# Latent attention: the score products of an even and an odd head issued next to each other

## The reference, cut to what matters

```
q = ln @ W_q
kv = jnp.concatenate([xn @ W_kv, ln @ W_kv], axis=1)
k, v = (kv[..., :INNER], kv[..., INNER:])
...
qn = rmsnorm(q, q_gamma) * SCALE
kn = rmsnorm(k, k_gamma)
sim = jnp.einsum('bhid,bhjd->bhij', qn, kn)
sim = jnp.where(full_mask[:, None, None, :], sim, neg)
attn = jax.nn.softmax(sim.astype(jnp.float32), axis=-1).astype(sim.dtype)
out = jnp.einsum('bhij,bhjd->bhid', attn, v)
...
return out @ W_out + b_out
```

## Time and profile before

| | |
|---|---|
| profiled execution, span | 1399.5 us |
| runs | 1397.72, 1401.20, 1401.49 us |
| mean granted TensorE clock | 0.864 of full speed |
| TensorE matmuls busy | 1089.6 us (78%) |
| VectorE / ScalarE / GpSimd busy | 810.9 / 577.6 / 535.3 us |
| score products (L1332), 128 matmuls | 52.7 us busy, 514 ns each |
| latent attention, first to last score | 864.5 to 1050 us |

### The profile page before, as it was taken

One profiled execution on the slowest core, in us unless ns is written; L12 is line 12 of the kernel. 1 busy time (PEld: TensorE's weight loads), 2 busy tenths in 40 slices (PEclk: granted clock), 3 DMA queues, 4 the chain that ended last, 5 costly groups with the idle time before them and its releaser, 6 DMA issues. The chain is left out here.

```text
span 1399.5 us, 27510 instructions
## 1 busy us (share of the span) xinstructions
PE 1089.6 (78%) x8779; PEld 824.4 (59%) x8789; DVE 810.9 (58%) x1770; ACT 577.6 (41%) x1366; POOL 535.3 (38%) x654
## 2 busy tenths in 40 slices
PE   5784968966598878506999348899998689997998
PEld 3564857855366666405999224566677367776443
DVE  4556624437647787673555353445454538775876
ACT  2442325432256655342434045554541247774000
POOL 1453734447147766380000433222220247763000
PEclk9755989988699999657999758899998789997999
DMA  3453268843221111276777120000000100000000
GB/s 105 115 148 121 102 206 292 291 146 95 77 89 41 36 44 35 83 275 220 260 257 251 59 73 1 0 1 0 1 0 9 38 8 21 16 16 5 15 22 23
DMA packets 71899, 125.99 MB, mean 90 GB/s; under 512 B 15737, under 2 KB 42499, under 8 KB 71811
## 3 DMA queue, kind: packets, MB, share of 16 engines
q1 hardware_dynamic: 64131, 103.88, 22.7%
q0 software_dynamic: 7680, 20.98, 4.5%
HBM read 53.38 MB, written 25.17 MB: 56 GB/s over the span
## 5 line engine op out<-in xcount | busy, mean ns | idle before, releaser
L297 ACT ACTIVATE xnT<-bank 128x256 f32<-128x256 f32 (+1 forms) x112 | 42.0, 380 | 85.9 <-PE bank L286 85.1
L1622 DVE TENSOR_REDUCE l2x_neg_max<-bank 128x1 f32<-128x333 f32 x64 | 32.0, 503 | 74.7 <-PE bank L1334 74.5
L3064 PE MATMUL bank<-l_weights,room 128*128 x576 | 70.1, 275 | 2.3 <-DVE room L3092 2.1
L3051 PE MATMUL bank<-room,xnT 128*128 128x128 bf16 x1152 | 69.7, 221 | 0.0
L3051 PEld LDWEIGHTS bank<-room,xnT 128*128 128x128 bf16 x1152 | 67.9, 99 | 0.3
L2712 POOL DMA_DIRECT2D l_results<-keep x24 | 13.1, 546 | 139.9 <-DVE keep L2810 139.9
L2326 PE MATMUL bank<-l0f_x_high,l_weights 128*128 128x256 bf16 x256 | 44.8, 300 | 27.7 <-DVE l0f_x_low L2351 16.8
L869 PE MATMUL bank<-ident,l_weights 128*77 128x128 f32 x256 | 39.5, 296 | 32.9 <-DVE l_weights L1060 27.6
L2165 DVE SCALAR_TENSOR_TENSOR l3f_total<-bank,l3f_share,l3f_total 128x256 f32<-128x256 f32 x112 | 54.2, 484 | 15.6 <-PE bank L2083 12.0
L3064 PEld LDWEIGHTS bank<-l_weights,room 128*128 128x128 bf16 x576 | 53.9, 97 | 13.2 <-issue 3.6
L2548 PE MATMUL bank<-l0r_xT_high,l0r_placed 128*128 128x128 bf16 x640 | 61.4, 221 | 0.0
(11 more groups left out here) (435 smaller groups left out, 3409.3 us busy)
## 6 DMA issues: line engine op xcount, KB each, us to landing
xnT<-l_weights SPq DMA_DIRECT2D x24, 1024.0 KB, 5.2
l0r_placed<-l_weights SPq DMA_DIRECT2D x40, 512.0 KB, 3.3
room<-in_L_ffn_weights SPq DMA_DIRECT2D x20, 512.0 KB, 4.6
l0w_staging<-in_L_ffn_weights SPq DMA_DIRECT2D x16, 480.0 KB, 3.9
l_weights<-in_L_ffn_weights SPq DMA_DIRECT2D x16, 384.0 KB, 3.2
l0r_room<-l_rows SPq DMA_DIRECT2D x40, 128.0 KB, 2.8
l_results<-l0r_room POOLq DMA_DIRECT2D x40, 128.0 KB, 2.8
l_rows<-l_weights SPq DMA_DIRECT2D x16, 192.0 KB, 2.3
```

The lines of the kernel that those rows point to most:

```text
L297: act.activation(self.chip.xnT[:, :, span(t, P)], bank[:, 0:DIM].rearrange("p (k n) -> p k n", k=KD), ACT.Copy).then_inc(self.copied, 1)
L3051: last = pe.matmul(h_bank[u][:, m * P:(m + 1) * P], placed.parts[w][:, u, at:at + P], x[:, u, k, :], start=(s == 1), stop=(s == PARTS * KD))
L3064: last = pe.matmul(bank[:, 2 + u, 0:DIM], h[:, u, c * P:(c + 1) * P], expert_part(split[:, w, :, :], e, KD * hidden_width + c * DIM, DIM), ...
```

## The change

Instead of `scores` at every step, TensorE issues `score_pair` at the even steps: the products of head s and head s + 1 next to each other (the one on partitions 0 to 63, the other on 64 to 127), then both mask products. The wait ahead of them is for the exponents of step s - 1 instead of s - 2. At odd steps TensorE issues no score. This holds for the prologue and for the loop; VectorE, ScalarE and GpSimd keep their programs.

```
-            def scores(b, s):
-                u, h = s // L2_HEADS, s % L2_HEADS
+            def score_pair(b, s):
+                u = s // L2_HEADS
                 if s == 0:
                     pe.wait_ge(qkT_ready, 2 * TPB * b + 2 * TPB)
                     pe.wait_ge(c_kT_placed, (KD + 1) * b + KD + 1)
-                wait(pe, probs_ready, SH * b + s - 1)
-                at = slice(L2_HEAD * (h % 2), L2_HEAD * (h % 2) + L2_HEAD)
-                pe.matmul(s_bank[h % 2][:, 0:L2_KEYS], qT[at, h // 2, u * P:(u + 1) * P], kT[at, h // 2, :],
-                          start=True, stop=False)
-                pe.matmul(s_bank[h % 2][:, 0:KEYS], mask_one[at, :], mask_now[at, :],
-                          start=False, stop=True).then_inc(scores_ready, 1)
+                wait(pe, probs_ready, SH * b + s)
+                halves = [slice(L2_HEAD * n, L2_HEAD * n + L2_HEAD) for n in range(2)]
+                pair = (s % L2_HEADS) // 2
+                for n, at in enumerate(halves):
+                    pe.matmul(s_bank[n][:, 0:L2_KEYS], qT[at, pair, u * P:(u + 1) * P], kT[at, pair, :],
+                              start=True, stop=False)
+                for n, at in enumerate(halves):
+                    pe.matmul(s_bank[n][:, 0:KEYS], mask_one[at, :], mask_now[at, :],
+                              start=False, stop=True).then_inc(scores_ready, 1)
...
             for s in range(SH):
-                scores(0, s)
+                if s % 2 == 0:
+                    score_pair(0, s)
...
                     if ahead >= 1:
-                        scores(b + 1, s)
+                        if s % 2 == 0:
+                            score_pair(b + 1, s)
```

## The result

The changed kernel takes 1442.27 us (median of 4 runs, 1424.47 to 1446.03) against 1399.46 us for the kernel before: 1.026 times as long, 95% interval 1.021 to 1.032. The ratio leaves out the slowest of the four runs (1446.03), which lay in a slower state of the chip, so it is less than the quotient of the two medians. The forecast had the sign, but its 13 us are a third of what came, and the time lies outside its range of 1395 to 1432. The profiled execution has a span of 1441.4 us, 41.9 more than before.

The account below looks back on a forecast made before the run. TensorE was taken as the bound in the steady latent attention, by its own work and order. Order +6 and clock +7 made +13 us: span 1399.5 to 1412.5, median 1401.2 to 1414; own range 1406 to 1422, wider range 1395 to 1432.

Parts of the forecast that it names:

- Two heads side by side cost what one costs: Scores on TensorE: four passes 0.86 us against 0.82 for one head's two; up to 28 x 0.79 = 22 us saved.
- The new wait eats the slots, section by section: Loop batches: pairs wait for the previous step's exponents; sections gain 0.2, gain 0.7, lose 1.15, gain 0.3 us: about 0.
- The prologue's +4.5: Prologue: nothing covers the pairs' waits, so score 0 of the loop starts at 888.8 instead of 884.26; bounds 3 to 5.
- The end of the batch: Score 6 to the next score 0: a chain through exponents, copies and place_qkT takes 6.3 us instead of 6.58, gain 0.3.
- The sum for "the next" batch: A second full loop batch, with gain 0.05 in its first section and loss 1.5 in section 4 to 6: +0.55 us.
- I take a quarter: +7 us: Clock term: falls to 1.2 GHz at TensorE's new gaps, 25 us over seven batches and 2.5 in the prologue, weighted down.
- the rival with a fall in every batch: Clock falls in section 4 to 6 of every batch, 3.6 us each: 1434, or 1424 with falls in most; chance 0.17.
- The price of a fall, 3.6 us: Per batch at 1.2 GHz: 2.0 us more from score 0 to 1, some 1.6 from pair 6 to next score 0.
- The last batch: End of the loop: said only that it has no scores; no term was given for it.
- The second to last batch: Batch without projections: three sections gain up to 0.79 us each, section 4 to 6 goes from 4.69 to 5.45; together -1.5.
- order +6: Sum without the clock: prologue 4.5, first batch 1.5, five batches 1.2, second to last -1.5, giving +5.7, say +6 us.
- The Trainium skill's rule on PSUM emptying: Packing the array speeds up TensorE but not PSUM emptying; narrower form: VectorE's and ScalarE's order and two banks bind, not throughput.

Follow-up runs that it names:

- the filled kernel: The changed kernel plus 12 unread products on TensorE ahead of the pair of steps 6 and 7 in every loop batch: 1400.3 us, ratio 1.0015.
- the two filled kernels: The changed kernel with 12 unread products ahead of pair 6 and 7, in every loop batch (1.0015) or only the last pass with scores (1.0167).
- the kernel with maximum 5 early: The changed kernel with VectorE finding maximum 5 right behind maximum 4, ahead of normalise, rms_norm, update_x and rms_sums: 1398.6 us, ratio 0.998.
- the one with the wait alone: The kernel before with single scores, but at even steps the score waits for the exponents of the step just before: 1433.3 us, ratio 1.023.
- the fills: 12 unread products ahead of score 6 in every loop batch, added to the changed kernel (ratio 1.0015) or the one with the wait alone (1.013).
- the one with the fill only in the last pass: The changed kernel plus 12 unread products ahead of the pair of steps 6 and 7, only in the last pass with scores: 1417.8 us, ratio 1.0167.

## Why the prediction was wrong

- *Two heads side by side cost what one costs:* right, 0.83 us for four passes, and each slot is worth 0.75 us where nothing waits.
- *The new wait eats the slots, section by section:* right. The three sections at full clock came within 0.05 us, and at full clock a batch takes 24.4 to 25.3 us, by the filled kernel. The prologue's +4.5 was met exactly, but partly by luck: its first wait cost 1.2 us less than forecast and the next section 1.4 more, and part of it ran at the low clock. With the same prologue the two filled kernels took 22.4 and 22.2 us there instead of 24.2, and more in the first batch instead (25.8 and 25.1 instead of 24.5). Prologue and first batch together lost 5.1 us in the changed kernel, where 6.0 were forecast.
- *The end of the batch* was worked out as 6.3 us for full clock and never ran so in the steady batches of the changed kernel. Where the clock held, in the filled kernel, it took 5.88, against 6.58 to 6.81 in the kernel before, so the end gains 0.7 to 0.9 us and not 0.3.
- The sum for "the next" batch was added up wrongly: its own terms, -0.05 - 0.7 + 1.5 - 0.3, give +0.45 and not +0.55. It changes nothing.
- *"I take a quarter: +7 us"* is the step that failed. It was a mean over falling and not falling, and no row gave the quarter. In the trace the clock fell in six of seven passes. The prediction had worked out the price of a fall in every batch (25 us), and the rows had already shown a fall after a gap of 1.1 us, where the new gap was twice that; so the rival with a fall in every batch deserved more than its chance. But a fall in every batch isn't certain: where the wait was filled in every batch or taken away, the traces have none to three batches with a fall, and the changed kernel's quickest run (1424.47 us, at a mean clock of 0.847 where the others have 0.830 to 0.832) probably had fewer; it has no trace.
- *The price of a fall, 3.6 us,* was too small: a batch with a fall takes 30.7 us where it takes 25.3 without, so 5.4, since pair 0 to 2 lost 2.2 us (8.32 against 6.15) and pair 6 to 0 lost 3.2 (9.08 against 5.88).
- *The last batch* was not in the sum at all. "The last batch has no scores" was taken for "nothing changes there"; it inherits the clock, and that cost 13 us by the ratios and 15 to 17 by the traces.
- The second to last batch was to gain 1.5 us. Its sections were 3.30, 3.78 and 5.47 us (before 3.60, 4.70, 4.69): the third is what was said (5.45), but up to its last pair the batch gained 0.4 us where the terms give 0.8. Its gap of 1.64 us was followed by the fall that the last batch kept.

By the terms: order +6 forecast, and about +5 by what the clock leaves of the 41.9 us (the filled kernel's ratio of 1.0015 holds -2 to +7 us); clock +7 forecast, about +37 found, of which some 21 in the five steady batches and 15 to 17 from the second to last batch on. The rival with a fall in every batch had the right mechanism and place, but too small a price and no last batch (1434, chance 0.17).

The Trainium skill's rule on PSUM emptying that was weighed ahead of the result ("TensorEngine Tiling (Array Packing)", section PSUM Bottleneck) held in the narrower form: VectorE and ScalarE were busy for 12.7 and 12.6 of a batch's 24.5 us in the kernel with maximum 5 early, and moving that one maximum undid the loss.

## What to carry to other kernels

When work is fused into pairs, fuse the consumers too: a pair that fills both buffers waits for the second consumer, wherever that stands in its engine's order. Look for the single instruction that stands behind a tail, here a row maximum of 0.50 us. And where a change leaves TensorE idle at one place of a loop that it kept busy before, price the fall of the clock in full, for every pass and for the stretch behind the loop, and set that beside the sum without falls instead of adding a share of it.

## What the runs showed of the hardware

- The clock can settle into the loop's own rhythm. Both kernels with the late wait ran batches of 30.7 us (30.68 and 30.70 in the changed one, 30.71 and 30.72 in the one with the wait alone), though one issues half as many score slots as the other. Without a fall they differ (25.3 and 26.5 to 26.8 with the fills). Why the period should be the same was not tried.
- TensorE can show as busy for 25.00 of 25.00 us and stay at 1.2 GHz. The last batch's transposes and products did so in the changed kernel; nearly the same work, entered at 2.4 GHz, kept that clock in the kernel before (14.20 us for 122 products where the slow stretch has 116) and in the one with the fill only in the last pass (1.00 from 1064 to 1083 us).
- An idle time of the same length is not always followed by a fall. In the kernel before the clock fell behind 1.1 us (876.2 to 877.3); in the first batch of the changed kernel it held behind 1.11 us, twice (ahead of the pairs at 898.04 and 904.70). Behind 1.87 us it fell within the next section in the changed kernel (933.49) and only at the end of it in the kernel with the fill in the last pass (921.11).
- Twelve products per batch that nobody reads, 1.47 us of them, brought the ratio from 1.026 to 1.0015, some 35 us.
